# Holding the splits of the next x until h is normalised, and splitting the second pair's transposes first

## The reference, cut to what matters

```
# layer 0, graph sum:  Wi, Wj = the two halves of W
mi  = x @ Wi.T ;  mj = x @ Wj.T ;  deg = adj.sum(axis=1)
g   = deg[:, None] * (mi + b) + adj @ mj
h   = layernorm(x + g)
# layer 1, masked attention with 8 heads of 64
q, k, v = h @ Wq.T + bq, h @ Wk.T + bk, h @ Wv.T + bv
p   = softmax(where(adj == 0, -inf, q @ k.T / 8))
out = layernorm(h + (p @ v) @ Wo.T + bo)
```

## Time and profile before

| what | us |
|---|---|
| median of 3 runs | 3231.28 (3230.65 to 3232.95) |
| the profiled execution | 3233.8 |
| its span, first to last instruction | 3232.0 |
| PE busy | 3082.5 (95%) |
| DVE busy | 2266.2 (70%) |
| ACT busy | 1670.3 (52%) |
| POOL busy | 1159.1 (36%) |
| granted TensorE clock, mean | 0.991 of full |
| DMA | 108.36 MB, 34 GB/s |

### The profile page before, as it was taken

One profiled execution on the slowest core, in us unless ns is written; L12 is line 12 of the kernel. 1 busy time (PEld: TensorE's weight loads), 2 busy tenths in 40 slices (PEclk: granted clock), 3 DMA queues, 4 the chain that ended last, 5 costly groups with the idle time before them and its releaser, 6 DMA issues.

```text
span 3232.0 us, 59563 instructions
## 1 busy us (share of the span) xinstructions
PE 3082.5 (95%) x20480; PEld 2689.6 (83%) x20480; DVE 2266.2 (70%) x5644; ACT 1670.3 (52%) x4487; POOL 1159.1 (36%) x1097
## 2 busy tenths in 40 slices
PE   6999999999999999999999999999999999999996
PEld 5888888888888888888888888888888888888886
DVE  5676776767767767777677677676776776767765
ACT  3555555555555454555555554554555545545554
POOL 2333333333333433333333333333333343333332
PEclk8999999999999999999999999999999999999998
DMA  3101101011011010110110110101101101101000
GB/s 124 34 20 39 38 21 39 19 39 39 19 39 39 19 39 26 32 39 19 39 39 19 39 39 19 39 19 39 39 19 39 39 19 39 33 26 39 19 33 20
DMA packets 73002, 108.36 MB, mean 34 GB/s; under 512 B 3600, under 2 KB 36880, under 8 KB 72976
## 3 DMA queue, kind: packets, MB, share of 16 engines
q1 hardware_dynamic: 72976, 108.02, 10.1%
HBM read 74.46 MB, written 33.55 MB: 33 GB/s over the span
## 4 chain that ended last, share of the span: by engine, by line
PE 77%; DVE 16%; issue 6%; DMA 0%; ACT 0%; POOL 0%; DVEq 0%; SPq 0%; POOLq 0%
PE proj L338 60%; PE attn L465 6%; PE av L338 6%; DVE pT_lo L792 5%; DVE h L845 4%; PE attn L477 4%; DVE stats_h L834 2%; DVE oT L802 2%; DVE h L820 1%; DVE hb L826 1%; DVE mean_var_h L840 0%; DMA hb<-in_w0T 0%; DMA xb<-in_x 0%; ACT probs L611 0%; POOL xb L259 0%
## 5 line engine op out<-in xcount | busy, mean ns | idle before, releaser
L611 ACT ACTIVATE probs<-probs,exp_bias 128x256 f32<-128x256 f32 x1024 | 509.8, 502 | 275.1 <-DVE exp_bias L783 275.1
L281 POOL TENSOR_TENSOR oT_lo<-oT,oT_hi 128x256 fp32r<-128x256 f32 x256 | 188.6, 737 | 1260.8 <-ACT oT_hi L642 1260.8
L627 ACT CAST pT_hi<-attn 128x512 fp32r<-128x512 f32 x512 | 275.8, 590 | 424.9 <-PE attn L477 423.4
L792 DVE TENSOR_TENSOR pT_lo<-attn,pT_hi 128x512 fp32r<-128x512 f32 x512 | 328.0, 682 | 213.7 <-ACT pT_hi L627 211.7
L248 POOL TENSOR_TENSOR probs<-probs,row_inv 128x512 f32<-128x512 f32 x256 | 264.1, 1042 | 441.3 <-DVE row_inv L788 441.1
L635 ACT COPY o_part<-av 64x512 f32<-64x512 f32 x256 | 149.7, 585 | 514.7 <-PE av L338 514.7
L777 DVE CUSTOM_DVE_ANT_0 probs<-attn,mask_add 128x256 f32<-128x256 f32 x1024 | 372.8, 421 | 54.7 <-PE attn L465 44.0
L802 DVE SCALAR_TENSOR_TENSOR oT<-av,bv_cols,o_part 64x256 f32<-64x256 f32 x512 | 243.3, 475 | 190.7 <-ACT o_part L635 180.7
L338 PE MATMUL av<-pT_hi,v_both 128*128 128x256 f32 x1024 | 274.7, 300 | 102.6 <-DVE pT_lo L792 99.1
L338 PE MATMUL proj<-mj_hi,wq_hi 128*128 128x256 f32 x1024 | 296.9, 290 | 1.5 <-DVE mj_lo L737 1.5
L338 PEld LDWEIGHTS av<-pT_hi,v_both 128*128 128x128 f32 x1024 | 195.6, 191 | 121.8 <-DVE pT_lo L792 112.9
(11 more groups left out here) (98 smaller groups left out, 8655.5 us busy)
## 6 DMA issues: line engine op xcount, KB each, us to landing
xT_raw<-in_xT SPq DMA_DIRECT2D x64, 512.0 KB, 4.5
xb<-in_x SPq DMA_DIRECT2D x64, 512.0 KB, 5.3
out<-hb SPq DMA_DIRECT2D x64, 512.0 KB, 3.3
probs<-in_w0T SPq DMA_DIRECT2D x1, 1024.0 KB, 6.6
hb<-in_w0T SPq DMA_DIRECT2D x1, 1024.0 KB, 8.8
probs<-in_wqT SPq DMA_DIRECT2D x1, 1024.0 KB, 5.8
hb<-in_wkT SPq DMA_DIRECT2D x1, 1024.0 KB, 7.2
probs<-in_wvT SPq DMA_DIRECT2D x1, 1024.0 KB, 5.5
```

What stands on the lines that cost most here:

```text
L281: pool.tensor_tensor(oT_lo[:, g, :], oT[:, :], oT_hi[:, g, :].bitcast(F32), ALU.subtract).then_inc(o_split, 1)
L611: last = nc.scalar.activation(e, e, ACT.Exp, bias=exp_bias[:, g % 2, s:s + 1], scale=SCALE, accum_out=row_sum[:, g % 2, s:s + 1])
L627: nc.scalar.copy(pT_hi[:, g % 2, i, :, :], attn[2 * (g % 2) + i][:, :].rearrange("p (k q) -> p k q", k=R)).then_inc(pt_hi_done, 1)
L792: V.tensor_tensor(pT_lo[:, g % 2, i, :, :], attn[2 * (g % 2) + i][:, :].rearrange("p (k q) -> p k q", k=R), pT_hi[:, g % 2, i, :, :].bitca ...
```

## The change

Two edits in the order of work, and no work added or taken away.

On POOL, the two instructions that split x of batch b + 2 have stood right behind the inverse root of h of batch n. Now a wait for the normalised h stands between. On ACT and DVE the split of the transposed probabilities of pair 1 moves ahead: on ACT ahead of the copy of attend 0's lower half (`o_low_part(b, 0)`), on DVE ahead of `y_sum(b - 1, 0)` and `o_sum(b, 0)`. PE's order and SP's order are the same as before, and so is `last_step`.

```diff
@@ POOL, step
                 root("h", n)
+                if ahead: pool.wait_ge(normed["h"], R * (n + 1))
                 if ahead: xT_high(b + 2)
                 if ahead: split_xT(b + 2)
                 split_o(b, 0)
@@ ACT, step
                 pt_high(b, 0, 1, not y_)
-                o_low_part(b, 0, not y_)
                 pt_high(b, 1, 0, not y_)
                 pt_high(b, 1, 1, not y_)
+                o_low_part(b, 0, not y_)
                 hT_high(n, 0)
@@ DVE, step
                 norm_apply("h", n, h_row)
+                pt_low(b, 1, 0)
+                pt_low(b, 1, 1)
                 if y_: y_sum(b - 1, 0, other)
                 o_sum(b, 0, not y_)
-                pt_low(b, 1, 0)
-                pt_low(b, 1, 1)
                 if y_: y_sum(b - 1, 1, other)
```

## The result

The changed kernel takes 3102.36 us (median of 4 runs, 3101.71 to 3104.67), the kernel before 3232.11 in its runs by then: a ratio of 0.96, with an interval of 0.9583 to 0.9616. On another chip, later, it took 3102.07, the kernel before 3232.99 (0.9595, 0.9582 to 0.9608). The forecast was 3106.8, so the gain came out at 129.8 us where 124.5 was forecast. The profiled execution took 3101.74 us, its span is 3099.9.

The account below looks back on a forecast made before the run. PE bounds the kernel, stopping each step for pt_low because POOL's splits hold the norm of h. 61 steps at 1.97 us plus 4.3 for step 0 give 124.5 us less: 3106.8 us, range 3101 to 3120.

Parts of the forecast that it names:

- What bounds the kernel: PE, busy 95% of the span, stopped 1.52 us each step for pt_low, late because POOL's splits held the norm of h.
- the 1.97 us a step: Gain per step from pair 0's scores to pair 2's: 24.16 us with the splits, 22.19 without.
- step 62: Step of the old trace without splits of x: norm pair 1.00 us instead of 4.66, PE did not stop.
- The hold at no cost: POOL's wait for the norm delays its splits to about 1621.4 from 1620.27, ahead of split_o(b, 0); nobody pays.
- DVE beside the splits: pt_low, y_sum and o_sum, each with one operand in PSUM, run unhindered beside POOL's splits.
- the rival that went slower: POOL's splits hold pt_low and the sums as they held the norm; 0.4 us a step lost, 3256 us; chance 0.04.
- The order at nothing: New order on ACT and DVE worth nothing with the hold; without it 0, from 0.1 gained to 0.1 lost per step.
- step 0: First loop step, no y to cover the norm; own gain between 3.5 and 4.3 us, 4.3 taken.
- The sum: 61 steps at 1.97 = 120.2 us plus 4.3 for step 0: 124.5 us, giving 3106.8.
- PE without a stop might get a lower clock: Rival: one per cent less clock over the span adds 31 us, 3138 us; chance 0.02.
- The margins: Time to spare on DVE: 0.3 us at attend 1 and 1.06 us at q, for hT_low.
- the late reckoning: Latest times for ACT's copies and DVE's pt_low, y_sum, o_sum: o_sum ends by 1621.2, attend 1 needs it at 1621.53.

Follow-up runs that it names:

- The experiment with two SBUF inputs: Kernel before, with the norm of h written as SCALAR_TENSOR_TENSOR, its second input the inverse root broadcast from SBUF; 3297.54 us (1.0203).
- the statistics instructions: Changed kernel with 4, 5 or 6 bn_stats added on DVE each step ahead of o_sum(b, 0); 3185.13, 3222.96 and 3334.17 us.
- The hold of one split only: Changed kernel with POOL's wait moved down one instruction, so the first split runs beside the norm and the second is held; 3106.25 us (0.961).

## Why the prediction was right, point by point

**What bounds the kernel, and the 1.97 us a step**: right. Both came out of step 62, which was the experiment already made inside the trace of before. The first stretch is 22.19 us in the changed kernel, the value of step 62 to the hundredth.

**The hold at no cost**: right. POOL's splits end at 1553.85 in the middle step and `split_o(b, 0)` starts at 1556.02, 2.2 us later. That the splits start 0.24 and not 0.1 us behind the norm did not matter.

**DVE beside the splits**: right, `pt_low` 1.29 us for two, `y_sum` 0.68 and `o_sum` 0.95 for two; the rival that went slower is out. The experiment with two SBUF inputs shows where it would have held, and agrees with the reason I gave, one operand in PSUM. That reason is enough, but not needed: the statistics instructions with their one input in SBUF went free as well.

**The order at nothing**: right for the loop with the hold in place, 22.19 us with either order. I took it at nothing everywhere. In step 0 it is worth 0.84 us, and 1.24 of clock behind it, because no y stands there to cover the sums. Without the hold I gave 0, 0.1 at most per step; it is 0.06, and 5.9 us of clock that no step of my working had. That working also had PE wait only ahead of attend 1; `y_sum`, now behind the two `pt_low`, stopped it for 1.14 us ahead of the transposes.

**The sum**: 124.5 forecast. By spans it is 3232.0 - 3099.9 = 132.1 us, and the chain splits it. The steps from the scores of pair 2 in step 0 to the scores of pair 0 in step 62 took 3134.89 - 90.17 = 3044.7 us before and 3003.26 - 84.60 = 2918.7 after: 126.1 us, where I had 61 x 1.97 = 120.2. **The missing term is 5.9 us of clock.** In the kernel before, in four steps (the scores of pair 2 at 485.43, 1277.32, 2069.22 and 2861.12, 792 us or 16 steps apart), the second stretch took 26.7 us instead of 25.24. The chain of one of them, and busy time by stretch with the clock:

```profile
1277.32 2.47 PE attn L465 x22
1279.80 12.18 PE proj L338 x96
```

```profile
1276.00:1277.30 1.30, 1.19 (x10) 1.06 (x10) 1.30 (x4) 0.00 (x0) 0.00 (x0) 1.00 0.00 0
1277.30:1279.80 2.50, 2.50 (x26) 2.28 (x25) 1.60 (x8) 0.89 (x2) 0.73 (x1) 0.59 0.00 0
```

The clock falls right behind the stop of PE, and the scores take 2.47 us for 1.62. 4 x 1.48 = 5.9 us, and the changed kernel, which has no stop in the loop, has no such step. I had read the granted clock only as a mean of long stretches, 1.00, and asked whether PE without a stop might get a lower clock; the trace had the opposite in it. Of the rest, step 0 gave 24.25 - 20.48 = 3.8 where I had 4.3: the end of the attend was not as fast as I assumed, at a granted clock of 0.66 from 80 to 85 us. The start was 1.8 us shorter, which I do not put down to the change, since it has no edit there: the scores of step 0 started between 64.1 and 65.1 us in the nine other profiled executions with the start unchanged, and the end was 0.5 shorter. By medians the gain is 129.8 us, 5.3 over the forecast, which the missing term of the clock alone would make up.

**The margins** were of the right size for the late reckoning, but I overrated the need for them. With the copies of ACT starting as soon as four transposes are done, `o_sum` ended 1.4 us ahead of attend 1 (1552.40 against 1553.82). The hold of one split only shows that 1.56 us more for the norm is still free.

**What stays open.** How long a stop must be for the clock to fall. Without a fall in the loop were stops of 0.86 and 1.45 us, and the two of 1.14 and 0.31; with a fall in one of 16 steps one of 1.54; in two of five steps the pair of 0.32 and 1.54; in every step from step 2 on one of 2.07. The order is that of the idle time in a step (0.86, 1.45, 1.45, 1.54, 1.86, 2.07 us), but the kernels differ in more than the stop, and one run of the last was made. The few us that the parts ahead of and behind the loop differ by (74.45 to 77.08 us at the end) fall where the granted clock is below 1.00; whether the clock alone makes them, and what sets it there, was not tried.

## What to carry to other kernels

When an instruction takes several times as long as its twin elsewhere, look at what runs on the other of DVE and POOL at that moment: if DVE's reads two inputs from SBUF, or is a TENSOR_SCALAR from SBUF to SBUF, it may be waiting for POOL's, as the norm of h was (2339 ns for 544). Not everything that reads from SBUF is held: four statistics instructions took their usual 2.46 us beside a split. Putting the instruction that nobody waits for behind the other costs only a semaphore. Look for a step of the loop in which the suspect is missing: it prices the change before anything is built. And price a stop of PE by more than its length, since the matmuls behind it take longer as well: 1.16 us in all for a stop of 0.86 here, and more where the granted clock fell to 0.57 behind it.

## What the runs showed of the hardware that I had not expected

A stop of PE has a step in its price. With 1.45 us of stop a step the kernel takes 3222.96 us, with 2.07 us (a single run) 3334.17: 0.6 us more of stop cost 111 us in 61 steps, 1.8 us each, of which some 1.2 are, by subtraction, the lower clock behind the stop. Whether parting a stop helps is not shown: two stops of 1.14 and 0.31 us made no fall of the clock in the loop, but one of their sum, 1.45, made none either.

The hold between DVE and POOL works in both directions and on the smallest instruction: POOL's addition on two elements a partition took 2.15 us instead of 0.19 beside a DVE instruction with two SBUF inputs. DVE's statistics instructions, with one, are not held.
